# A Mamba layer and a table-coded FFN on one core: segment sums as pairs of fp16 products, and y transposed by a DMA

## The reference, cut to what matters

```python
x = x + _layernorm(mamba(_layernorm(x)))
x = x + _layernorm(ffn(_layernorm(x)))

# mamba, 8 heads of 64, state of 64
z, x, B_toks, C_toks, dt_toks = split(u @ W_in.T)
x, B_toks, C_toks = split(silu(conv4(x, B_toks, C_toks)))
A = -exp(A_log); dt = softplus(dt_toks + dt_bias); dA = exp(dt * A)
S = S * dA_t[:, :, None, None] + einsum('bh,bn,bhp->bhpn', dt_t, B_t, x_t)   # per token
y_t = einsum('bhpn,bn->bhp', S, C_t)
y = (ys + D_param * xh) * silu(z)
return y.reshape(Bb, Ll, D_MODEL) @ W_out.T

# ffn: weights are lut[idx], 16 values, 1376 wide
h = silu(x @ lut[gate_idx].T) * (x @ lut[up_idx].T);  return h @ lut[down_idx].T
```

## Time and profile before

| | us |
|---|---|
| median of 3 runs | 1443.71 (1440.67 to 1446.11) |
| the profiled execution, its own time | 1443.4 |
| its span, first to last instruction | 1441.7 |
| PE busy | 1361.3 |
| DVE, ACT, POOL busy | 933.8, 577.1, 457.6 |

### The profile page before, as it was taken

The page is one execution under the profiler, slowest core; times in us unless marked ns, Lnnn a source line. Parts: engine busy times, 40 slices in busy tenths (PEclk is TensorE's granted clock), DMA queues, the critical chain, the costliest instruction groups (busy, mean ns, idle before and its releaser), DMA issues. The chain is left out here.

```text
span 1441.7 us, 19103 instructions
## 1 busy us (share of the span) xinstructions
PE 1361.3 (94%) x6912; PEld 672.6 (47%) x6912; DVE 933.8 (65%) x1869; ACT 577.1 (40%) x1018; POOL 457.6 (32%) x691
## 2 busy tenths in 40 slices
PE   4878987988999999999999999999999999999998
PEld 2334444444554445444545445544554444444443
DVE  7978866987577656765676567755775555544432
ACT  5466655676444234332434243423442233122120
POOL 1312233333233434334322433254334242310102
PEclk9889998999999999999999999999999999999999
DMA  5133233322310223013301320032102110311201
GB/s 164 37 102 88 69 93 100 92 75 56 74 45 23 59 70 85 19 36 93 73 16 52 88 71 26 23 92 77 44 23 71 39 44 23 97 43 30 74 1 51
DMA packets 99021, 87.79 MB, mean 61 GB/s; under 512 B 68208, under 2 KB 68208, under 8 KB 98928
## 3 DMA queue, kind: packets, MB, share of 16 engines
q1 hardware_dynamic: 97040, 86.54, 21.8%
q10 hardware_dynamic: 1888, 0.03, 0.1%
HBM read 54.05 MB, written 16.78 MB: 49 GB/s over the span
## 5 line engine op out<-in xcount | busy, mean ns | idle before, releaser
L1312 PE MATMUL bank<-fxt,ffn_hi 128*128 128x512 f16 (+1 forms) x1408 | 418.8, 379 | 2.0 <-DVE dn L1677 1.5
L1312 PE MATMUL bank<-fxt,ffn_lo 128*128 128x512 f16 (+1 forms) x704 | 266.8, 379 | 0.0
L1312 PEld LDWEIGHTS bank<-fxt,ffn_hi 128*128 128x128 f16 (+1 forms) x1408 | 139.8, 100 | 173.1 <-issue 12.9
L1210 PE MATMUL bank<-mask,diag 128*128 128x416 f16 x640 | 128.0, 354 | 21.7 <-ACT ffn_lo L830 20.2
L605 POOL TENSOR_TENSOR state<-state,ex 64x512 f32<-64x512 f32 x32 | 36.8, 1149 | 343.3 <-PE bank L1265 342.3
L1326 PE MATMUL bank<-ffn_hi,h_hi 128*128 128x512 f16 (+1 forms) x352 | 133.5, 379 | 0.0
L1326 PE MATMUL bank<-ffn_hi,h_lo 128*128 128x512 f16 (+1 forms) x352 | 133.4, 379 | 0.0
L1326 PE MATMUL bank<-ffn_lo,h_hi 128*128 128x512 f16 (+1 forms) x352 | 133.3, 379 | 0.0
L1643 DVE SCALAR_TENSOR_TENSOR gact<-gact,bank 128x512 f32<-128x512 f32 (+1 forms) x88 | 60.2, 684 | 105.7 <-ACT gact L874 104.8
L874 ACT ACTIVATE gact<-bank,c_gate_half 128x512 f32<-128x512 f32 (+1 forms) x88 | 59.9, 681 | 154.7 <-PE bank L1312 153.1
L1496 DVE TENSOR_SCALAR mask<-codes_h 128x832 f16<-128x832 f16 x320 | 111.7, 408 | 12.5 <-PE bank L1210 12.2
(11 more groups left out here) (184 smaller groups left out, 2357.3 us busy)
## 6 DMA issues: line engine op xcount, KB each, us to landing
codes_sb<-codes SPq DMA_DIRECT2D x80, 208.0 KB, 3.4
ures<-u SPq DMA_DIRECT2D x32, 256.0 KB, 2.8
x_scratch<-x SPq DMA_DIRECT2D x32, 256.0 KB, 2.0
ut<-x_scratch SPq DMA_DIRECT2D x16, 512.0 KB, 4.3
xres<-x_scratch SPq DMA_DIRECT2D x32, 256.0 KB, 3.0
out<-dn SPq DMA_DIRECT2D x32, 256.0 KB, 2.1
ut<-u SPq DMA_DIRECT2D x15, 512.0 KB, 4.4
ffn_hi<-w_in_t SPq DMA_DIRECT2D x4, 580.0 KB, 9.2
```

Source lines behind the costliest of these rows:

```text
L1210: last = nc.tensor.matmul(p.bank[:, 0:COLS], diag[:, q].rearrange("p n m -> p (n m)"), mask[:, n, q, j * COLS:(j + 1) * COLS], start=(q == ...
L1312: last = nc.tensor.matmul(bank, wt[:, c0:c0 + w], fxt[:, :, half, k, :], start=(k == 0 and n == 0), stop=(k == KC - 1 and n == 2))
```

## The change

What it does:

- `da` is kept as a high and a low fp16 half, scaled by 256 and held above -60000 (three more small DVE steps per tile; `dt_steps` counts 21 instead of 18). The masks get fp16 copies.
- `segments`: two multiplies with fp16 inputs and outputs, one per half, into the same bytes of `decay`. `segment_sums`: four fp16 matmuls of 512 columns instead of two fp32 ones. The chunk sums: six fp16 matmuls of 8 columns instead of three fp32 ones. ACT's exponentials undo the scale.
- `transpose_y` goes from PE to SP, as one transposing DMA per chunk from `ysplit` to `yt`; `y_transposed` on ACT and the turns `y0` to `y3` go. `project_out` and DVE's step 10 of the next chunk wait for the DMA's landing. The DMA waits for DVE's step 11 and for the output projection before it.
- SP's order is written out for the decoding stages and for the others; each `transpose_y(t, c)` stands ahead of the store of the chunk before.

```diff
@@ sync
+                def transpose_y(t, c):
+                    sp.wait_ge(y_steps.sem, y_steps.now(t, YSTEPS * (c + 1)))
+                    if t > 0 or c > 0:
+                        last = place(t, f"o{c - 1}") if c > 0 else place(t - 1, f"o{SUB - 1}")
+                        sp.wait_ge(last.filled, last.n + 1)
+                    y_turned.inc(sp.dma_start_transpose(yt[:].rearrange("p n k t -> p (n k) t"),
+                                                        ysplit[:].rearrange("p n d -> p (n d)")))
...
+                def stage(t):
+                    g = t - LAG
+                    nxt = t + 1 < TILES
+                    transpose_y(t, 0)
+                    if nxt:
+                        transpose_pair("u", t + 1, 0)
+                        load_pair("u", t + 1, 1)
+                    store_x1(t - 1, 3)
+                    residual(t, 0)
+                    if nxt:
+                        transpose_pair("u", t + 1, 1)
+                    load_pair("x", t - 1, 0)
+                    transpose_y(t, 1)
+                    store_x1(t, 0)
+                    residual(t, 1)
+                    transpose_y(t, 2)
+                    store_x1(t, 1)
+                    residual(t, 2)
+                    load_xres(g, 0)
+                    transpose_pair("x", t - 1, 0)
+                    load_pair("x", t - 1, 1)
+                    transpose_y(t, 3)
+                    store_x1(t, 2)
+                    residual(t, 3)
+                    store_out(g, 0)
+                    load_xres(g, 1)
...
@@ gpsimd, segments
-                        pool.wait_ge(dt_steps.sem, dt_steps.now(t, 17))
-                    seg_ready.inc(nc.gpsimd.tensor_tensor(
-                        decay[:], causal[:].unsqueeze(1).broadcast_to((P, HEADS, P)),
-                        da[:, t % HALVES, c, :].unsqueeze(2).broadcast_to((P, HEADS, P)), ALU.mult))
+                        pool.wait_ge(dt_steps.sem, dt_steps.now(t, 20))
+                    for n in range(2):
+                        seg_ready.inc(nc.gpsimd.tensor_tensor(
+                            segs[:, n], causal_h[:].unsqueeze(1).broadcast_to((P, HEADS, P)),
+                            da[:, t % HALVES, c, n, :].unsqueeze(2).broadcast_to((P, HEADS, P)), ALU.mult))
@@ scalar
-                def y_transposed(t, c):
-                    p = place(t, f"y{c}")
-                    act.wait_ge(p.filled, p.n + 1)
-                    nc.scalar.activation(
-                        yt[:], p.bank[:].bitcast(F16).rearrange("p (n k t) -> p n k t", n=2, k=KC), ACT.Copy).then_inc(p.freed, 1)
@@ tensor
-                    for n, sums in enumerate((causal, below, ones)):
-                        last = nc.tensor.matmul(p.bank[:, 192 + n * HEADS:192 + (n + 1) * HEADS], sums[:],
-                                                da[:, half, c, :], start=True, stop=True)
+                    for n, sums in enumerate((causal_h, below_h, ones_h)):
+                        for piece in range(2):
+                            last = nc.tensor.matmul(p.bank[:, 192 + n * HEADS:192 + (n + 1) * HEADS], sums[:],
+                                                    da[:, half, c, piece, :], start=(piece == 0), stop=(piece == 1))
...
-                        last = nc.tensor.matmul(seg_banks[n][:], below[:],
-                                                decay[:, 4 * n:4 * n + 4, :].rearrange("p h t -> p (h t)"),
-                                                start=True, stop=True)
+                        for piece in range(2):
+                            last = nc.tensor.matmul(seg_banks[n][:], below_h[:],
+                                                    segs[:, piece, 4 * n:4 * n + 4, :].rearrange("p h t -> p (h t)"),
+                                                    start=(piece == 0), stop=(piece == 1))
...
-                def transpose_y(t, c):
-                    p = take(t, f"y{c}")
-                    pe.wait_ge(y_steps.sem, y_steps.now(t, YSTEPS * (c + 1)))
-                    to = p.bank[:].bitcast(F16).rearrange("p (n k t) -> p n k t", n=2, k=KC)
-                    for n in range(2):
-                        for k in range(KC):
-                            last = nc.tensor.transpose(to[:, n, k, :], ysplit[:, n, k * P:(k + 1) * P], ident_h[:])
-                    last.then_inc(p.filled, 1)
...
-                    y_place = place(t, f"y{c}")
-                    pe.wait_ge(y_place.freed, y_place.n + 1)
+                    pe.wait_ge(y_turned.sem, y_turned.now(t, c + 1))
@@ vector, time_steps
-                        da[:, p], dt[:], a_sb[:].unsqueeze(1).broadcast_to((P, SUB, HEADS)), ALU.mult))
+                        dtp[:], dt[:], a_sb[:].unsqueeze(1).broadcast_to((P, SUB, HEADS)), ALU.mult))
+                    chain(dt_steps, i, 18, nc.vector.tensor_scalar(dtp[:], dtp[:], SEG_LOW, None, ALU.max))
+                    chain(dt_steps, i, 19, nc.vector.tensor_copy(da[:, p, :, 0, :], dtp[:]))
+                    chain(dt_steps, i, 20, nc.vector.tensor_sub(da[:, p, :, 1, :], dtp[:], da[:, p, :, 0, :]))
```

More of the change, by code:

```diff
@@ L163, in sandwich_kernel @@
         causal = sb("causal", [P, P])
-        below = sb("below", [P, P])
-        ones = sb("ones", [P, P])
+        causal_h = sb("causal_h", [P, P], F16)
+        below_h = sb("below_h", [P, P], F16)
+        ones_h = sb("ones_h", [P, P], F16)
         neg_half = sb("neg_half", [P, SUB])
@@ L495, in stage @@
-                    if t >= 1 and g < 0:
+                    load_codes(k + 22)
+                    load_codes(k + 23)
+                    if t >= 1:
                         transpose_pair("x", t - 1, 0)
-                    if g >= 0:
-                        store_out(g, 0)
-                        load_xres(g, 1)
-                        store_out(g, 1)
-                        load_xres(g, 2)
-                    if t >= 1:
-                        transpose_pair("x", t - 1, 1)
+                        transpose_pair("x", t - 1, 1)
@@ L504, in stage @@
                     if t + 2 < TILES:
                         load_pair("u", t + 2, 0)
[L506 to L512 removed]
+                    store_out(g, 2)
+                    load_xres(g, 3)
+                    store_out(g, 3)
                 def tail(t):
@@ L539, in _ @@
                     load_codes(k)
-                for t in range(TILES):
+                for t in range(LAG):
+                    decode_stage(t)
+                for t in range(LAG, TILES):
                     stage(t)
@@ L704, in _ @@
                 nc.gpsimd.memset(causal[:], 1.0).then_inc(s_fill, 1)
-                nc.gpsimd.memset(below[:], 1.0).then_inc(s_fill, 1)
-                nc.gpsimd.memset(ones[:], 1.0).then_inc(s_fill, 1)
+                nc.gpsimd.memset(below, 1.0).then_inc(s_fill, 1)
+                nc.gpsimd.memset(ones_h[:], 1.0).then_inc(s_fill, 1)
                 nc.gpsimd.memset(neg_half[:], -0.5).then_inc(s_fill, 1)
@@ L1622, in y_split @@
                     if t > 0 or c > 0:
-                        before = place(t, f"y{c - 1}") if c > 0 else place(t - 1, f"y{SUB - 1}")
-                        dve.wait_ge(before.filled, before.n + 1)
+                        dve.wait_ge(y_turned.sem, y_turned.now(t, c))
                     y_step(t, c, 10, nc.vector.tensor_scalar(ysplit[:, 0, :], y[:], yq[:], None, ALU.mult), count)
@@ L1955, in _ @@
                 dve.wait_ge(s_alog, 1)
-                step(nc.vector.tensor_scalar(a_sb[:], a_sb[:], -1.0, None, ALU.mult))
+                step(nc.vector.tensor_scalar(a_sb[:], a_sb[:], -SEG, None, ALU.mult))
                 conv(0, 4)
```

106 lines of the change are left out of this document (46 added, 60 removed).

## The result

| | before | after |
|---|---|---|
| median, us (6 runs each) | 1444.14 (1440.01 to 1446.11) | 1433.84 (1431.17 to 1437.78) |
| ratio, 95% interval | | 0.993 (0.991 to 0.995) |
| the profiled execution, its own time | 1443.4 | 1433.2 |
| its span | 1441.7 | 1431.1 |

The account below looks back on a forecast made before the run. PE was taken as the bound, 94% busy and fully busy in stages 2 to 6. Gains of 38.6 (stages 2 to 6), 7.5 (stage 7) and 15 us (stages 0 and 1) sum to 61: 1383 us, range 1368 to 1402.

Parts of the forecast that it names:

- What each piece costs PE: Per chunk on PE: segment sums gain 0.94 us, chunk sums 0.54, y's transposes 0.45; 1.93 together, 61.7 over 32 chunks.
- The DMA for y: SP's transposing DMA, taken to land in 3.5 us (2.0 to 5.4), hides before the output projection, with at least 4.8 left.
- The third rival: SP's transpose of y lands late and the output projection waits: 1499 us at a 16 us landing; chance 0.03.
- Stages 2 to 6, "no loss as long as nothing becomes late": 20 chunks where PE is always busy: all 38.6 us of removed PE work becomes time, as long as nothing becomes late.
- Three DVE steps of 0.2 us per tile, in the shadow: The three added DVE time steps per tile, 0.2 us each, were claimed to cost no time.
- Stages 0 and 1, half of 30 us: In the stages that decode FFN weights, 30 us could be gained at best; half, 15 us, was taken.
- 10.1 us of waits for y's copy: Stages 0 and 1: PE's waits for ACT's copy of y's transpose, 10.1 us, would be removed outright.
- 15.4 us of PE's work: Stages 0 and 1: the work taken from PE in 8 chunks, 15.4 us of the 30 at best.
- 4.5 us of half clock behind the y waits: Stages 0 and 1: PE's half clock behind two waits for y's copy, 4.5 us of the 30 at best.
- The first rival, "DVE sets stages 0 and 1": The mask chain and contention eat the gain in stages 0 and 1: 0, or 5 us lost; 1398 to 1403; chance 0.11.
- The prologue: Before the first scan: 2.5 us added by a multiply and DVE steps, offset by cheaper sums; about 0, 1 either way.
- the second rival: GpSimd's fp16 multiply costs twice, 3.8 us, losing the gain and ten more in stages 0 and 1; 1409 us; chance 0.04.

Follow-up runs that it names:

- e1: Only the y half of the change: y transposed by SP's DMA, with the old fp32 sums and one GpSimd multiply; 1441.9 us, 0.998 of before.
- e3: The changed kernel with one GpSimd multiply per chunk, low halves of the segment terms left out, PE's work the same; 1414.9 us, 0.979 of before.
- e4: The changed kernel with DVE's time steps in stages 2 to 6 moved from ahead of the seventh gate to ahead of the ninth; 1419.5 us, 0.983 of before.
- e7: e4 with nine idle PE products in each of the 8 chunks of stages 0 and 1, where y's transposes stood; 1410.6 us, 0.976 of before.
- e10: e5 with twice as many idle products in stages 0 and 1 (32, 28, 24 and 20 a stage); 1409.3 us, 0.978 of before.
- e11: e4 with DVE's masks made for half the columns and read twice, so the FFN weights are wrong; 1399.6 us, 0.969 of before.
- e5: e4 with 16, 14, 12 and 10 idle products ahead of PE's long waits in each of stages 0 and 1; 1410.4 us, 0.976 of before.
- e9: The kernel before the change with the same idle products as e5 and nothing else; 1452.6 us, 1.006 of before.

## Why the prediction was wrong, point by point

**What each piece costs PE: right.** Segment sums 0.87 us (0.86 forecast), chunk sums 0.16 (0.15), transposes 0.45 (e1). The steady stage of after without its 3.0 us idle is 145.2 us long (144.8 forecast). Stage 7 with the tails gained 8.3 us (7.5). The step from a matmul's duration to the distance of starts held: 1.8 us a steady stage in e1 for 4 x 8 transposes is 56 ns each. The 275 ns that the Trainium skill gives ("TensorE: Matmul & The Clock Gate", Part 4) would have made it 8.8; the run decides against it here.

**The DMA for y: right.** Issues of y's transposes in after (issue min/median/max in ns, start of the first and the last), and their landing in us:

```profile
L443 SPq DMA_TRANSPOSE yt<-ysplit x32: 1232/1239/1362, 82.5 to 1235.1; - x32
...
DMA to landing us min/median/max: 3.1/3.1/4.6
```

PE waits for none of them. The third rival did not occur.

**Stages 2 to 6, "no loss as long as nothing becomes late": this step failed, by 21.9 us.** The evidence for room was that stage 7 idles only 2.3 us with 26 us less work. The rows bear neither the 26 nor the comparison. The stretch of 132 us that they came from begins at 1119 us, 15 us before stage 7; from the first scan of stage 7 to its fourth PE is busy 96.1 of 97.3 us, against 110.1 of 110.1 in stage 3, so 14.0 us less. And stage 7 has no next tile, hence no convolution and no time steps on DVE, which are just what stands ahead of gact. The prediction itself said that DVE has less there too, and took it anyway; the slack of the feeder was a row away. In chunk 1 of stage 3 of before, DVE and then PE:

```profile
561.57 0.69 DVE L1595 TENSOR_TENSOR y<-bank,ex 128x512 f32<-128x512 f32 x1 [0.16 <-PE bank L1265]
...
566.16 0.66 DVE L1659 TENSOR_TENSOR h_lo<-hf,h_hi 128x512 f16<-128x512 f32 x1
...
572.71 2.33 DVE L1524 SCALAR_TENSOR_TENSOR xs<-cin,conv_w_sb,xs 128x512 f32<-128x512 f32 x3
...
585.75 0.66 DVE L1643 SCALAR_TENSOR_TENSOR gact<-gact,bank 128x512 f32<-128x512 f32 x1
...
587.68 0.59 PE L1312 MATMUL bank<-fxt,ffn_hi 128*128 128x512 f16 x2
```

gact is done at 586.41 and PE comes for it at 587.68: 1.3 us of slack, while the change lets PE come 1.93 us earlier. The same steps in after, with GpSimd's multiplies:

```profile
570.77 0.69 DVE L1610 TENSOR_TENSOR y<-bank,ex 128x512 f32<-128x512 f32 x1 [0.31 <-PE bank L1291]
...
575.37 1.74 DVE L1673 TENSOR_TENSOR h_lo<-hf,h_hi 128x512 f16<-128x512 f32 x1
...
582.95 2.99 DVE L1536 SCALAR_TENSOR_TENSOR xs<-cin,conv_w_sb,xs 128x512 f32<-128x512 f32 x3
...
596.38 0.66 DVE L1657 SCALAR_TENSOR_TENSOR gact<-gact,bank 128x512 f32<-128x512 f32 x1
...
572.81 3.75 POOL L603 TENSOR_TENSOR decay<-causal_h,da 128x1024 f16<-128x1024 f16 x2 [0.80 <-PE bank L1295]
...
597.10 0.61 PE L1328 MATMUL bank<-fxt,ffn_hi 128*128 128x512 f16 x2 [1.96 <-DVE gact L1657]
```

From the scan's first step to gact it is 24.2 us before and 25.6 after. Longer are: h_lo by 1.08, which starts under the second multiply and ends 0.5 us behind its end; the three new time steps, 0.66 in all; the convolution's steps by 0.66, now beside GpSimd's xdt and xd (from 584.32 us), which before began at 574.69, 0.4 us ahead of their end. That is 2.4 us and, with 0.2 of a smaller step, 2.6; DVE lost in exchange a wait of 1.2 us for ACT's decays (at 578.26 before), so 1.4 arrive at gact. e3, with one multiply, has both of the held steps back at their old length:

```profile
568.90 0.66 DVE L1673 TENSOR_TENSOR h_lo<-hf,h_hi 128x512 f16<-128x512 f32 x1
...
575.45 2.33 DVE L1536 SCALAR_TENSOR_TENSOR xs<-cin,conv_w_sb,xs 128x512 f32<-128x512 f32 x3
```

With these terms, 1.9 earlier and 1.4 later against 1.3 of slack make the wait of 2.0. Together with 0.9 in chunk 0 this is the 3.0 us a stage, 14.9 in five. "Three DVE steps of 0.2 us per tile, in the shadow" and the contention counted for stages 0 and 1 alone were thus both wrong: here they had no cover. e4 and e3, which take one each away, bring the stage to 145.9 and 146.9.

Stages 4 to 6 lose 1.7 us each on top, by the clock: it falls in the wait, and PE runs 3.4 us at the lower level behind it, where each microsecond does half the work. In stages 2 and 3 the same wait of 2.0 us was followed by no fall. The matmul behind the wait in stage 4, and the window that it opens:

```profile
745.29 1.02 PE L1328 MATMUL bank<-fxt,ffn_hi 128*128 128x512 f16 x2 [2.09 <-DVE gact L1657]
```

```profile
745.30:755.00 9.70, 9.70 (x38) 4.05 (x39) 5.87 (x9) 3.00 (x6) 1.01 (x4) 0.82 0.00 0
```

14.9 of waits and 5.1 of clock are 20.0 of the 21.9; the rest is 0.4 us a stage by which the work of PE came out above 144.8.

The Trainium skill has the contention ("GPSIMD Engine Reference", Specifications: DVE instructions with two SBUF inputs contend with GpSimd for SBUF). The trace agrees for h_lo (1.74 us against 0.66). What it costs is a matter of where such a step stands, which only the rows tell.

**Stages 0 and 1, half of 30 us: this step failed, by 28.8 us, in its sign.** The three terms of the 30 went so:
- *10.1 us of waits for y's copy, "removed outright"*: the named waits went, the idle time did not (e1: 44.2 to 44.6 us). A wait's name says which of several near-equal feeders was last. ACT's wait row went from 20.2 to 41.5.
- *15.4 us of PE's work*: PE's busy time there rose by 1.8 us (266.0 to 267.7), because 41 more us of it ran at half clock. By e7, which gives the work back, this costs 9 us and not 0.
- *4.5 us of half clock behind the y waits*: not gained; half clock went from 44 to 85 us.

So the step that failed is the taking of half of 30 us as gained: the clock costs about 9 us of the 13.8 (e7), and e10 shows that the chunks which lost most come back with the clock. The other 5 us, what remains between e7 and before, are open. GpSimd's second multiply (4.3 us in e3) may be in them, but e3 also had 20 us less half clock, so the 4.3 and the clock's 9 can't be added; and e1 loses 9.4 us without a second multiply. Nor do the runs say why the removed waits were replaced in full, or what SP's new order and the three time steps on DVE do there, which no run took out alone. The first rival, "DVE sets stages 0 and 1", had the direction and far too small a price (0 to 5 lost for all it named, 14 measured); it had no term for the clock, although the clock of 0.91 and 0.94 was in the rows that the forecast began with.

**The prologue: 0.5 us lost, within the 1 of its bounds.** The bounds can't be judged by that: with one and the same prologue the first scan began between 61.5 us (e11) and 63.0 (e5). The wait for the first terms grew by 3.5 us, from 4.0 to 7.5, where 2.5 were counted.

**GpSimd's multiply: right.** The group of after; with fp16 in and out it costs what the fp32 one did, 1.91 us, so the second rival (twice) did not occur:

```profile
L603 POOL TENSOR_TENSOR decay<-causal_h,da 128x1024 f16<-128x1024 f16 x64 | 120.9, 1911 | 28.6 <-PE bank L1295 23.0
```

**The range.** It allowed stages 0 and 1 to lose 5 us and stages 2 to 6 nothing. A range for a bound that had 0 us idle should have asked what each feeder's slack is. And for stages 0 and 1 the rows showed waits, a clock under 1 and three engines near the bound, so that the loss there needed a rival of its own, of the size of the gain.

## What to carry to other kernels

When the bounding engine is 100% busy, taking work from it is worth only as much as the smallest slack of what feeds it: look up, for each handover in a period, when the feeder ended and when the bound engine came, and add the feeder's own new work (here 1.3 us of slack against 1.9 + 1.4). A named wait that is removed in a stage with several engines near the bound is no gain until the total idle time falls. A stage in which PE waits can lose clock when its work gets lighter, as stages 0 and 1 did here: give the forecast a case in which the gain there is zero or negative, and move the new steps of the feeder behind its handover first (one moved call, e4, took the kernel from 1433.8 to 1419.5).

## What the runs showed of the hardware

- Less work for PE between waits went with more time at 1.2 GHz: with 15.4 us of work taken from two stages their time at the lower level was 85 us in place of 44. 36 useless fp16 matmuls a stage brought it to 51 us and the two stages down by 9 us (e4 to e7); filling of the same kind in the kernel before, which had 44 us to start with, made them 11 us longer in the profile and the kernel 3 to 13 us longer in ten executions (e9).
- A multiply of 128x1024 by GpSimd takes 1.91 us with fp16 as with fp32 operands.
- A DVE step with two inputs in SBUF (one fp32, one fp16) that started under such a multiply ended 0.5 us behind its end: 1.74 us instead of 0.66, and 0.66 again with one multiply (e3).
- The same program differs in its granted clock from one execution to the next: e1 from 0.968 (1447.6 us) to 0.979 (1431.0 us).
- A transposing DMA of 128x1024 fp16 within SBUF holds SP 1.24 us and lands in 3.1, of 128x2048 1.90 and 4.3: less than in proportion.
